# Causal attention on one Trainium2 core: the diagonal blocks become a unit of their own, with their masks on other engines

## The chip, the cores and the metric

The kernel runs on one core of a Trainium2 chip. The metric is the device time of one execution in microseconds (us). The core has a matmul engine (TensorE, "PE" in the profile, its weight loads "PEld"), three engines for elementwise work (VectorE "DVE", ScalarE "ACT", GpSimd "POOL") and queues that start DMA transfers ("SPq" is the one of SyncE). [...]

## The reference, cut to what matters

The program has four stages on x of 8 batches x 1024 tokens x 256 features: a banded attention, a mixture of experts, a causal attention ("attn_b"), and the experts again. Only the causal attention is touched:

```python
def _L0_attn_b_ref(x, W1, b1, W2, b2):
    y = jnp.einsum('bse,ef->bsf', x, W1) + b1            # B 8, S 1024, H 16 heads of 16
    y = y.reshape(B, S, H, -1).transpose(0, 2, 1, 3)
    q, k, v = jnp.split(y, 3, axis=-1)
    w = jnp.einsum('bhqd,bhkd->bhqk', q, k) / dk
    w = w * mask - NEG_BIG * (1.0 - mask)                # mask = tril
    w = jax.nn.softmax(w, axis=-1)
    attn = jnp.einsum('bhqk,bhkd->bhqd', w, v)
    ...
    return jnp.einsum('bse,ef->bsf', attn, W2) + b2
```

## The kernel before

The causal attention is `dense_attention`. It works in groups of 4 heads (HG), 4 groups a batch, 32 groups in all. The 1024 x 1024 scores of a head are 8 x 8 tiles of 128 x 128, of which 36 matter. They are packed in "units" of 1024 columns, so that each unit fills one PSUM slot: five units for a head (the fifth, of 512 columns, is shared by two heads), 18 slots' worth for a group. `unit_tiles` says which key tiles lie in a unit of the transposed scores ("S"), `unit_maxima` which query tiles lie in a unit of the maxima pass ("mx").

Each group runs two passes over the scores. "mx" (L1193) computes queries x keys, so that VectorE's TENSOR_REDUCE (L1334) finds each query's maxima by tile. "mred" (L1304 to L1314) reduces these and splits the result in three bf16 parts, "mt" transposes them on TensorE (L1250), VectorE copies them (L1347), and "mrow" sends them by DMA (L1143) to three extra rows of `q_stack`. Then "S" (L1186) computes keys x queries minus the maximum, ScalarE takes the exponential (L1373) into `probs`, and "PV" (L1213) multiplies the values with them into `outT_ps`. PV's four heads write to four different groups of 17 of the array's columns; it is fp32, and each matmul has two records. In both passes every diagonal tile gets its mask by one more 128-column bf16 matmul that adds -1e30: `sooner` in S (L1189), `later` in mx (L1198).

The order of all work is one written-out list, `dense_schedule`. A group is 18 "beats"; each has one S step, up to one or two PV pieces, then the mx steps of the *next* group (18 of them spread over beats 0 to 14), and side work. "mred" is at beat 15, "mt" and "mrow" at beat 16. Side work by group of a batch: group 0 has the output of the batch before (ot, at, op: beats 4 to 8) and the layer norm and transposes of the next one (z, zt: beats 10 to 13), groups 1 and 3 project q and k of the next batch (from beat 6), group 2 its values. Every engine walks the list in order and skips what isn't its own.

S, mx and the side work share a ring of three PSUM slots (`slot_free`): a step may write when the step three before it has been taken out by VectorE or ScalarE. A projection's slot is taken twice: by ScalarE, which adds the bias and rounds to bf16 (L1387, part 0), and then by VectorE, which forms the remainder in `full` (L1341). ScalarE rounds that to part 1 (L1391), VectorE subtracts again for part 2 (L1319), and SyncE spills the three parts to DRAM, from where they are stacked.

A PV piece of unit u is put in the list from the first S step of unit u+1 on, one a beat, and its matmuls wait for the last exponential of unit u.

Of the kernel before, what the change touches and what calls it, by code (L numbers as in the profile page):

```python
# [844 lines left out]

UNITS = 5
# [5 lines left out]
def unit_tiles(u):  # L852

    return ((u, 0), (NT - u, N - P * u)) if 0 < u < 4 else ((0, 0),) if u == 0 else ((4, 0),)


def unit_maxima(u):

    return ((7 - u, 0), (u - 1, P * (NT - u))) if 0 < u < 4 else ((7, 0),) if u == 0 else ((3, 0),)


def dense_schedule():

# [16 lines left out]
    def maxima(b, g):  # L880
# [21 lines left out]
    def others(b, g):  # L902
# [25 lines left out]
    for b in range(B):  # L928
        for g in range(G):
# [5 lines left out]
            for n, step in enumerate(beat_units("S", b, g)):  # L935
# [5 lines left out]
                for _ in range(1 if u < 4 else 2):  # L941
# [10 lines left out]
def dense_attention(nc, x_sb, stats, ident, w, scratch):  # L952
# [4 lines left out]
    for name, kinds in {"filled": BY_DVE + BY_ACT, "taken_dve": BY_DVE, "taken_act": BY_ACT, "qk": ("q", "k"), **{kind: (kind,) for kind in (  # L957
            "S", "PV", "ote", "z", "mred", "part1", "part2", "mrow")}}.items():
# [29 lines left out]
    with ExitStack() as ctx:  # L988
# [11 lines left out]
        sooner = sb("sooner", [P, P], BF16)  # L1000
# [4 lines left out]
        with ExitStack() as setup:  # L1005
# [8 lines left out]
            with nc.Block() as block:  # L1014
# [20 lines left out]
                def _(pool):  # L1035
# [3 lines left out]
                    pool.memset(sooner[:, :], 0.0).then_inc(pool_steps, 1)  # L1039
                    pool.wait_ge(pool_steps, 3)  # L1040
# [5 lines left out]

                    pool.affine_select(out=sooner[:, :], in_=sooner[:, :], compare_op=ALU.is_ge, fill=NEG, base=0,
                                       pattern=[[1, P]], channel_multiplier=-1).then_inc(pool_steps, 1)
                    pool.wait_ge(pool_steps, 6)
# [29 lines left out]
        tops = sb("tops", [P, HG, 4 * NT + NT // 2])  # L1079
        neg_max = sb("neg_max", [P, HG, NT])  # L1080
# [11 lines left out]
        pv_done, ote_done, z_ready, mred_chain, mred_done, recip_done = (  # L1092
            sem(n) for n in ("pv_done", "ote_done", "z_ready", "mred_chain", "mred_done", "recip_done"))
        part0_done, part1_done, part2_done, mrows_in = (sem(n) for n in ("part0_done", "part1_done", "part2_done", "mrows_in"))
# [781 lines left out]
```

## Time and profile before

| | us |
|---|---|
| median of 3 runs | 3950.71 (3942.34 to 3953.79) |
| the profiled execution | 3953.15 |
| its span | 3951.4 |
| TensorE busy | 3270.7 (83%) |
| VectorE busy | 1763.2 (45%) |
| ScalarE busy | 1195.8 (30%) |
| GpSimd busy | 77.1 (2%) |

In the page's slices of the span, the causal attention is the second half up to about 3600 us, which starts at 1990 us; its steady part is 2030 to 3580 us. A busy time counts a matmul from its start to its modelled end, so that matmuls that follow each other closely overlap: the cost of one in a stream is read from start to start. "Idle before" is the time that the engine stood still ahead of a group of instructions, with what ended it.

### The profile page before, as it was taken

The page shows a single profiled execution, that of the slowest core. Times are in us where ns is not written, and L with a number is a line of the kernel's source. Part 1 is how long each engine was busy: PE and PEld are TensorE (multiplying, and loading weights), DVE is VectorE, ACT ScalarE, POOL GpSimd, SP SyncE. Part 2 cuts the span into 40 slices and gives each one's busy share as a digit, 9 for nine tenths or more (in the row PEclk, how much of TensorE's full clock was granted, in tenths as well). Part 3 has the DMA queues.
Part 4 walks back from the last instruction along what each step waited for, and adds up shares of the span by engine and source line. Part 5 has one row for each costly group of instructions (what it writes and reads, how often), then busy time and mean ns, then how long its engine had stood idle before and what let it go on. Part 6 is the DMA issues. An engine that isn't in the chain of part 4 may idle for free. (4 is left out here: it accounts for less than half of the span.)

```text
span 3951.4 us, 96618 instructions
## 1 busy us (share of the span) xinstructions
PE 3270.7 (83%) x43580; PEld 1868.0 (47%) x43580; DVE 1763.2 (45%) x3275; ACT 1195.8 (30%) x1486; POOL 77.1 (2%) x144
## 2 busy tenths in 40 slices
PE   1688888888888888789758888888888888887898
PEld 0466566656565656434524434343434343443345
DVE  5233343434333434430555555555555655563402
ACT  0122222222222222231024444444444444443300
POOL 0000000000000000000000000000000000000000
PEclk9678798878888878899679999999999999998997
DMA  5422223232223232239232222222222222202295
GB/s 129 101 68 68 71 71 79 65 82 62 74 62 79 58 81 61 90 140 415 57 80 49 49 49 49 49 49 49 49 49 49 49 49 49 49 17 89 82 418 186
DMA packets 235030, 343.13 MB, mean 87 GB/s; under 512 B 115962, under 2 KB 144452, under 8 KB 218244
## 3 DMA queue, kind: packets, MB, share of 16 engines
q1 hardware_dynamic: 222452, 334.40, 29.6%
q8 instruction: 340, 5.57, 0.6%
q10 hardware_dynamic: 12176, 2.66, 0.5%
q14 instruction: 62, 0.51, 0.0%
HBM read 266.15 MB, written 69.24 MB: 85 GB/s over the span
## 5 line engine op out<-in xcount | busy, mean ns | idle before, releaser
L1334 DVE TENSOR_REDUCE b_tops<-b_slot 128x8 f32<-128x1024 f32 x576 | 688.6, 1220 | 489.3 <-PE b_slot L1198 482.4
L1373 ACT ACTIVATE b_probs<-b_slot 128x1024 f32<-128x1024 f32 x576 | 584.1, 1022 | 581.1 <-PE b_slot L1189 396.2
L1186 PE MATMUL b_slot<-b_q_stack,b_k_stack 99*128 99x512 bf16 (+3 forms) x1536 | 389.8, 335 | 131.6 <-DMA b_q_stack<-b_neg_rows 71.2
L711 DVE TENSOR_TENSOR a_probs<-a_scores,a_bias_k 128x512 f32<-128x512 f32 x256 | 176.6, 690 | 559.5 <-PE a_scores L570 325.4
L1193 PE MATMUL b_slot<-b_k_stack,b_q_stack 96*128 96x512 bf16 (+3 forms) x1536 | 382.5, 341 | 30.5 <-DVE b_tops L1334 22.1
L1213 PE MATMUL b_outT_ps<-b_probs,b_v 128*17 128x512 f32 (+3 forms) x3072 | 333.3, 514 | 22.2 <-ACT b_probs L1373 22.2
L803 ACT ACTIVATE a_probs<-a_probs 128x512 f32<-128x512 f32 x256 | 161.5, 631 | 592.6 <-DVE a_probs L711 591.4
L1186 PEld LDWEIGHTS b_slot<-b_q_stack,b_k_stack 99*128 99x128 bf16 x1536 | 138.4, 100 | 299.9 <-DMA b_q_stack<-b_neg_rows 93.9
L1193 PEld LDWEIGHTS b_slot<-b_k_stack,b_q_stack 96*128 96x128 bf16 x1536 | 120.3, 100 | 291.2 <-issue 174.5
L1189 PE MATMUL b_slot<-b_sooner,b_ident 128*128 128x128 bf16 x1024 | 227.5, 222 | 0.0
L1198 PE MATMUL b_slot<-b_later,b_ident 128*128 128x128 bf16 x1024 | 209.0, 223 | 0.0
L1747 PE MATMUL f_ps<-f_w_ring,f_hidT 128*32 128x256 f32 x1024 | 184.0, 381 | 2.1 <-ACT f_hidT L1788 2.1
L576 PE MATMUL a_aux<-a_k_stack,a_q_stack 96*64 96x64 bf16 x2048 | 162.2, 313 | 8.1 <-issue 8.1
L631 PE MATMUL a_outT_ps<-a_probs,a_v_near 128*17 128x64 f32 (+1 forms) x8448 | 164.8, 239 | 4.5 <-issue 4.4
L576 PEld LDWEIGHTS a_aux<-a_k_stack,a_q_stack 96*64 96x64 bf16 x2048 | 138.1, 219 | 50.2 <-issue 50.1
L658 PE MATMUL a_aux<-a_zT,a_wqk 128*128 128x512 f32 x256 | 159.6, 782 | 0.8 <-ACT a_zT L831 0.8
L576 PE MATMUL a_scores<-a_q_stack,a_k_stack 99*64 99x64 bf16 x2048 | 159.7, 313 | 0.0
L631 PEld LDWEIGHTS a_outT_ps<-a_probs,a_v_near 128*17 128x17 f32 x8448 | 143.1, 110 | 27.5 <-issue 18.3
L1726 PE MATMUL f_ps<-f_w_ring,f_lhs 128*32 128x512 f32 x512 | 146.8, 601 | 7.9 <-POOL f_lhs L1710 7.9
L763 DVE TENSOR_REDUCE a_far_max<-a_aux 128x8 f32<-128x512 f32 x128 | 88.4, 692 | 137.3 <-PE a_aux L576 137.3
L651 PE MATMUL a_aux<-ident,a_zb 128*128 128x128 f32 x128 | 28.5, 369 | 140.3 <-DVE a_zb L719 140.3
L576 PEld LDWEIGHTS a_scores<-a_q_stack,a_k_stack 99*64 99x64 bf16 x2048 | 137.1, 219 | 13.7 <-issue 4.1
(211 smaller groups left out, 4126.0 us busy)
## 6 DMA issues: line engine op xcount, KB each, us to landing
f_w_ring<-in_L_ffn_w_dram SPq DMA_DIRECT2D x128, 1024.0 KB, 9.4
parts_dram<-a_parts SPq DMA_DIRECT2D x96, 256.0 KB
parts_dram<-b_parts SPq DMA_DIRECT2D x96, 256.0 KB
a_k_stack<-parts_dram SPq DMA_DIRECT2D x128, 128.0 KB, 3.0
b_k_stack<-parts_dram SPq DMA_DIRECT2D x64, 256.0 KB, 6.9
a_q_stack<-parts_dram SPq DMA_DIRECT2D x64, 192.0 KB, 3.0
b_q_stack<-parts_dram SPq DMA_DIRECT2D x32, 384.0 KB, 4.7
values_dram<-a_v_stage SPq DMA_DIRECT2D x32, 272.0 KB, 2.9
```

The costliest lines, as they stand in the source:

```text
L576: ins = pe.matmul(dst[RES * r2:RES * (r2 + 1), 64 * pair:64 * (pair + 1)], left[rows, h, r:N:LINKS], right[rows, h, r:N:LINKS], start=star ...
L631: ins = pe.matmul(outT_ps[BLK * h:BLK * h + HD + 1, lo:top], v_near[g % 2][:, c, blk % 4, (HD + 1) * h:(HD + 1) * (h + 1)], probs[h][:, at ...
L711: dve.tensor_tensor(dst[:, :].rearrange("p (t c) -> p t c", c=64), src[:, :].rearrange("p (t c) -> p t c", c=64), bias_k[k][:, HG * g + h, ...
L803: act.activation(dst[:, :], dst[:, :], ACT.Exp).then_inc(probs_ready, 1)
L1186: ins = pe.matmul(dst[:, at:at + top - lo], k_stack[n][:, head, mine], q_stack[n][:, head, lo:top], start=True, stop=not own, skip_group_c ...
L1189: ins = pe.matmul(dst[:, at:at + P], ident16[:, :], sooner[:, :], start=False, stop=True, skip_group_check=True)
L1193: ins = pe.matmul(dst[:, at:at + top - lo], q_stack[n][0:QK_ROWS, head, mine], k_stack[n][0:QK_ROWS, head, lo:top], start=True, stop=not o ...
L1198: ins = pe.matmul(dst[:, at_own:at_own + P], ident16[:, :], later[:, :], start=False, stop=True, skip_group_check=True)
L1213: ins = pe.matmul(outT_ps[32 * h:32 * h + HD + 1, lo:hi], v1[b % 2][:, j, HG * g + h, :], src[:, base + lo - P * j:base + hi - P * j], sta ...
L1334: ins = dve.tensor_reduce(out, src, AX.X, ALU.max)
L1373: act.activation(probs_of(b, g, u, h)[:, :], slot_of(step)[:, :], ACT.Exp).then_inc(taken_act, 1)
L1747: ins = pe.matmul(bank[4 + half][32 * j:32 * j + 32, 0:D], hidT[half][:, c, j, :], w2_ring[:, j, c, :], start=c == 0, stop=c == HE // P - 1)
```

## The change

The units of both passes are cut anew. Unit 0 is now the eight diagonal tiles of a head, side by side; units 1 to 4 hold only tiles off the diagonal (in S unit 1 holds key tiles 0 and 6, and so on). What follows from it:

- S has no mask matmuls. In its unit 0 GpSimd sets what lies above the diagonal to zero in `probs`, after the exponential, with one affine_select of 128 x 1024 for each head; PV pieces of unit 0 wait for these ("masked").
- mx has its masks in unit 0 alone: two matmuls of 512 columns with `later` broadcast, ahead of the eight blocks. The reduction by tile gives diagonal and other maxima apart, and mred joins them with one more instruction.
- PV of unit 0 is 8 tiles x 4 heads of 128 columns, in two pieces. PV pieces come one at each beat but a unit's first (in the last unit, one and two).
- The 18 mx steps are spread over beats 0 to 12, mred is at beat 13, mt and mrow at 15.
- A projection's slot is taken once, by VectorE, into `full` (with the bias). ScalarE rounds `full` to part 0, GpSimd subtracts it from `full` ("rest1"), ScalarE makes part 1, GpSimd part 2. Projections start at beat 5, with six steps for each of q and k, where it was 6 with four.
- VectorE waits for all memsets once, ahead of its first step.

The diff, cut:

```diff
 def unit_tiles(u):
-    return ((u, 0), (NT - u, N - P * u)) if 0 < u < 4 else ((0, 0),) if u == 0 else ((4, 0),)
+    return ((u - 1, 0), (7 - u, N - P * u)) if u < 4 else ((3, 0),)
 def unit_maxima(u):
-    return ((7 - u, 0), (u - 1, P * (NT - u))) if 0 < u < 4 else ((7, 0),) if u == 0 else ((3, 0),)
+    return ((NT - u, 0), (u, N - P * u)) if u < 4 else ((4, 0),)
...
-            out += [(which, b, half), ("part1", b, half, which), ("part2", b, half, which), ("spill", b, half, which)]
+            out += [(which, b, half)] + [(step, b, half, which) for step in ("part0", "rest1", "part1", "part2", "spill")]
...
-            out[n * (BEATS - 3) // len(units)].append(step)
-        out[BEATS - 3].append(("mred", b, g))
-        out[BEATS - 2] += [("mt", b, g), ("mrow", b, g)]
+            out[n * (BEATS - 5) // len(units)].append(step)
+        out[BEATS - 5].append(("mred", b, g))
+        out[BEATS - 3] += [("mt", b, g), ("mrow", b, g)]
...
+        if u == 0:
+            return [("PV", b, g, 0, n, 512 * n, 512 * n + 512) for n in range(2)]
...
-            for lo, hi in ((P * j, 512), (max(512, P * j), N)):
+            for lo, hi in ((P * (j + 1), 512), (max(512, P * (j + 1)), N)):
...
-                put(projections(b + 1, g // 2), 6)
+                put(projections(b + 1, g // 2), 5)
...
-                for _ in range(1 if u < 4 else 2):
+                for _ in range((h > 0) if u < 4 else 1 + h):
...
+                for step in seq:
+                    if step[0] == "S" and step[3] == 0:
+                        _, b, g, u, h = step
+                        pool.wait_ge(taken_act, count("taken_act", *step))
+                        blocks = probs_of(b, g, u, h)[:, :].rearrange("p (j q) -> p j q", q=P)
+                        pool.affine_select(out=blocks, in_=blocks, compare_op=ALU.is_ge, fill=0.0, base=0,
+                                           pattern=[[0, NT], [1, P]], channel_multiplier=-1).then_inc(masked, 1)
+                    elif step[0] == "rest1":
+                        pool.wait_ge(part0_done, count("part0", "part0", b, half, which))
+                        pool.tensor_tensor(full[:, :], full[:, :], parts["qk".index(which)][:, 0, :], ALU.subtract).then_inc(rest1_done, 1)
+                    elif step[0] == "part2":
+                        pool.wait_ge(part1_done, count("part1", "part1", b, half, which))
+                        pool.tensor_tensor(parts[m][:, 2, :], full[:, :], parts[m][:, 1, :], ALU.subtract).then_inc(part2_done, 1)
...
+                        if u == 0:
+                            for c in range(2 if kind == "mx" else 0):
+                                pe.matmul(dst[:, 512 * c:512 * (c + 1)], ident16[:, :], later[:, :].unsqueeze(1).to_broadcast([P, 4, P]),
+                                          start=True, stop=False, skip_group_check=True)
+                            for tile in range(NT):
+                                mine = slice(P * tile, P * tile + P)
+                                ins = pe.matmul(dst[:, mine], own[0:rows, h, mine], other[0:rows, h, mine], start=kind == "S", stop=True,
+                                                skip_group_check=True)
...
-                                        if own:
-                                            ins = pe.matmul(dst[:, at:at + P], ident16[:, :], sooner[:, :], start=False, stop=True,
-                                                            skip_group_check=True)
...
+                        if u == 0:
+                            pe.wait_ge(masked, HG * (b * G + g + 1))
...
+                dve.memset(neg_off[:, :, :], -LOWEST).then_inc(cleared, 1)
+                dve.wait_ge(cleared, N_CLEARED)
...
-                        for u in range(UNITS):
+                        for u in range(1, UNITS):
...
+                        dve.wait_ge(mred_chain, n + 1)
+                        dve.scalar_tensor_tensor(out=neg_max[:, :, :], in0=tops[:, :, 0:NT], scalar=-1.0, in1=neg_off[:, :, :],
+                                                 op0=ALU.mult, op1=ALU.min).then_inc(mred_chain, 1)
...
-                            dve.wait_ge(part0_done, count("qk", *step))
-                            ins = dve.scalar_tensor_tensor(out=full[:, :], in0=src[:, :], scalar=bqk[:, m, half:half + 1],
-                                                           in1=parts[m][:, 0, :], op0=ALU.add, op1=ALU.subtract)
+                            ins = dve.tensor_scalar(full[:, :], src[:, :], bqk[:, m, half:half + 1], None, ALU.add)
...
+                        act.wait_ge(taken_dve, count("taken_dve", which, b, half))
+                        act.activation(parts[m][:, 0, :], full[:, :], ACT.Copy).then_inc(part0_done, 1)
```

## Rows read from the trace of the kernel before

**Rows 1.** Busy time in stretches: us, PE, PEld, DVE, ACT, POOL, PEclk, DMA share, GB/s

```profile
1990.00:2032.00 42.00, 29.38 (x88) 16.00 (x88) 13.15 (x17) 13.73 (x13) 0.00 (x0) 0.78 0.36 87
...
2030.00:3520.00 1490.00, 1282.72 (x8956) 594.27 (x8956) 856.20 (x1186) 666.75 (x662) 0.00 (x0) 0.96 0.23 50
```

**Rows 2.** Waits of PE from 2030 to 3520 us: total, times, longest

```profile
PE b_slot L1186 <- DMA b_q_stack<-b_neg_rows: 67.4, 30, 3.2
PE b_slot L1186 <- DVE b_full L1341: 42.9, 28, 1.5
PE b_slot L1193 <- DVE b_tops L1334: 21.7, 76, 0.4
PE b_outT_ps L1213 <- ACT b_probs L1373: 17.6, 36, 0.6
PE b_slot L1186 <- DVE b_tops L1334: 15.7, 39, 0.5
...
PE b_slot L1250 <- DVE b_neg_parts L1314: 12.7, 8, 4.3
```

**Rows 3.** Timeline of PE, 2602 to 2604 us: start, length, instruction

```profile
2602.39 0.22 PE L1198 MATMUL b_slot<-b_later,b_ident 128*128 128x128 bf16 x1
2602.45 0.22 PE L1193 MATMUL b_slot<-b_k_stack,b_q_stack 96*128 96x128 bf16 x1
...
2603.13 0.38 PE L1186 MATMUL b_slot<-b_q_stack,b_k_stack 99*128 99x512 bf16 x1
2603.34 0.22 PE L1189 MATMUL b_slot<-b_sooner,b_ident 128*128 128x128 bf16 x1
```

**Rows 4.** Timeline of PE around two value products, 2614 to 2617 us

```profile
2614.22 1.05 PE L1213 MATMUL b_outT_ps<-b_probs,b_v 128*17 128x512 f32 x8
...
2615.21 0.50 PE L1193 MATMUL b_slot<-b_k_stack,b_q_stack 96*128 96x512 bf16 x2
...
2616.42 0.41 PE L1213 MATMUL b_outT_ps<-b_probs,b_v 128*17 128x128 f32 x8
...
2616.76 0.45 PE L1193 MATMUL b_slot<-b_k_stack,b_q_stack 96*128 96x512 bf16 x2
```

**Rows 5.** Timeline of DVE: the first maxima alone, then a remainder and mred

```profile
2033.34 20.45 DVE L1334 TENSOR_REDUCE b_tops<-b_slot 128x8 f32<-128x1024 f32 x18 [7.25 <-PE b_slot L1198]
...
2622.84 1.28 DVE L1341 SCALAR_TENSOR_TENSOR b_full<-b_slot,b_bqk,b_parts 128x1024 f32<-128x1024 f32 x1 [2.96 <-PE b_slot L1198]
...
2631.38 0.72 DVE L1304 TENSOR_REDUCE b_neg_max<-b_tops 128x4 f32<-128x32 f32 x8
```

**Rows 6.** Timeline of PE: after a projection, then a group's end and the next start

```profile
2624.18 0.39 PE L1186 MATMUL b_slot<-b_q_stack,b_k_stack 99*128 99x512 bf16 x1 [1.53 <-DVE b_full L1341]
...
2629.65 0.38 PE L1193 MATMUL b_slot<-b_k_stack,b_q_stack 96*128 96x512 bf16 x1
...
2631.75 1.27 PE L1213 MATMUL b_outT_ps<-b_probs,b_v 128*17 128x128 f32 x16 [0.56 <-ACT b_probs L1373]
2633.04 0.26 PE L1250 MATMUL b_slot<-b_ident,b_neg_parts 128*96 128x128 bf16 x1
...
2636.73 0.61 PE L1186 MATMUL b_slot<-b_q_stack,b_k_stack 99*128 99x512 bf16 x1 [2.11 <-DMA b_q_stack<-b_neg_rows]
```

**Rows 7.** Timeline of ACT: a projection's part 0, then an exponential

```profile
2621.64 1.11 ACT L1387 ACTIVATE b_parts<-b_slot,b_bqk 128x1024 bf16<-128x1024 f32 x1 [4.09 <-PE b_slot L1231]
2622.65 1.02 ACT L1373 ACTIVATE b_probs<-b_slot 128x1024 f32<-128x1024 f32 x1
```

**Rows 8.** Groups of POOL over the whole span: busy us, mean ns, idle before

```profile
L490 POOL TENSOR_TENSOR a_far_parts<-a_spread,a_far_parts 128x256 bf16<-128x256 f32 x32 | 21.4, 670 | 2.6
...
L107 POOL TENSOR_SCALAR_AFFINE_SELECT ident<-ident 128x128 f32<-128x128 f32 x1 | 0.3, 295 | 0.2 <-POOL ident L105 0.2
```

**Rows 9.** Stretches of PE before and after a group's start: us, busy, PEclk, DMA share, GB/s

```profile
2634.00:2636.00 2.00, 0.62 (x8) 1.00 0.27 89
...
2638.00:2640.00 2.00, 2.00 (x9) 0.50 0.96 200
```

More of the change, by code:

```diff
@@ L957, in dense_attention @@
     for name, kinds in {"filled": BY_DVE + BY_ACT, "taken_dve": BY_DVE, "taken_act": BY_ACT, "qk": ("q", "k"), **{kind: (kind,) for kind in (
-            "S", "PV", "ote", "z", "mred", "part1", "part2", "mrow")}}.items():
+            "S", "PV", "ote", "z", "mred", "part0", "rest1", "part1", "part2", "mrow")}}.items():
         for step in seq:
@@ L1038, in _ @@
                     pool.memset(later[:, :], 0.0).then_inc(pool_steps, 1)
-                    pool.memset(sooner[:, :], 0.0).then_inc(pool_steps, 1)
-                    pool.wait_ge(pool_steps, 3)
+                    pool.wait_ge(pool_steps, 2)
                     pool.affine_select(out=ident16[:, :], in_=ident16[:, :], compare_op=ALU.not_equal, fill=1.0, base=0,
@@ L1045, in _ @@
                                        pattern=[[-1, P]], channel_multiplier=1).then_inc(pool_steps, 1)
-                    pool.affine_select(out=sooner[:, :], in_=sooner[:, :], compare_op=ALU.is_ge, fill=NEG, base=0,
-                                       pattern=[[1, P]], channel_multiplier=-1).then_inc(pool_steps, 1)
-                    pool.wait_ge(pool_steps, 6)
+                    pool.wait_ge(pool_steps, 4)
                 @block.scalar
@@ L1175, in _ @@
                         dst = slot_free(step)
-                        heads = ((h, 0),) if u < 4 else ((2 * h, 0), (2 * h + 1, 512))
-                        for head, base in heads:
+                        own, other, rows = (k_stack[n], q_stack[n], ALL_ROWS) if kind == "S" else (q_stack[n], k_stack[n], QK_ROWS)
+                        if u == 0:
[6 more added lines that the diff above has]
+                                                skip_group_check=True)
@@ L1178, in _ @@
+                        for head, base in ((h, 0),) if 0 < u < 4 else ((2 * h, 0), (2 * h + 1, 512)) if u else ():
                             for tile, at in (unit_tiles if kind == "S" else unit_maxima)(u):
                                 at += base
-                                mine = slice(P * tile, P * tile + P)
-                                lo, end = (P * tile, N) if kind == "S" else (0, P * tile + P)
+                                lo, end = (P * tile + P, N) if kind == "S" else (0, P * tile)
@@ L1200, in _ @@
+                                    ins = pe.matmul(dst[:, at:at + top - lo], own[0:rows, head, P * tile:P * tile + P],
+                                                    other[0:rows, head, lo:top], start=True, stop=True)
                                     at, lo = at + top - lo, top
@@ L1203, in _ @@
                         _, b, g, u, n, lo, hi = step
-                        first = step == ("PV", b, g, 0, 0, 0, 512)
-                        pe.wait_ge(taken_act, count("taken_act", "S", b, g, u, HG - 1 if u < 4 else HG // 2 - 1))
-                        if first:
+                        begins = u == 0 and n == 0
+                        if u == 0:
+                            pe.wait_ge(masked, HG * (b * G + g + 1))
+                        else:
+                            pe.wait_ge(taken_act, count("taken_act", "S", b, g, u, HG - 1 if u < 4 else HG // 2 - 1))
+                        if begins:
                             if prev := before(b, g):
@@ L1314, in _ @@
                         dve.tensor_tensor(neg_parts[:, 2, :, :], neg_max[:, :, :], neg_parts[:, 1, :, :], ALU.subtract).then_inc(mred_done, 1)
-                    elif kind == "part2":
-                        _, b, half, which = step
-                        m = "qk".index(which)
-                        dve.wait_ge(part1_done, count("part1", "part1", b, half, which))
-                        dve.tensor_tensor(parts[m][:, 2, :], full[:, :], parts[m][:, 1, :], ALU.subtract).then_inc(part2_done, 1)
                     elif kind == "stats":
```

60 lines of the change are left out of this document (26 added, 34 removed).

## Prediction

> **What bounds the kernel now.** I read the busy times by stretch first, to see which engine is nearest to full in the causal attention. From 2030 to 3520 us TensorE is busy 1283 of 1490 us, VectorE 856, ScalarE 667, GpSimd not at all [rows 1]. So TensorE's own work and its idle time set this stage, and the other stages are untouched. Then I read the waits of TensorE: what stopped it, by releaser [rows 2]. The largest is the start of a group, where S waits for the DMA that brings the negated maxima: 67.4 us in 30 groups, 2.25 us each. Next is the slot of a projection, which two engines take out in turn: 42.9 us, 28 times 1.53 us. Then the slot ring, where a step waits for VectorE's reduction of the step three before: 21.7 + 15.7 = 37.4 us, 1.2 us a group. The first value product of a unit waits for an exponential: 17.6 us. The transpose of the maxima waits for mred: 12.7 us, of which the first group has 4.3 and seven others 1.2 each.
>
> Third, the timeline, for what an instruction costs in a stream (start to start, not its length). A mask of 128 columns starts at 2602.39 and the next matmul at 2602.45: 0.06 us. A block of 512 columns takes 0.21 (2603.13 to 2603.34) [rows 3]. A PV piece of four heads takes 0.99 us for 512 columns and 0.34 for 128 [rows 4]. By these, each group has 18 S steps, 18 mx steps and twelve PV pieces on TensorE. VectorE's reductions back to back take 20.45/18 = 1.14 us each [rows 5], so the 18 of a group need 20.5 us of the 46 that a group lasts.
>
> Fourth, the granted clock. TensorE's clock is at 2.4 GHz most of the time, but the wait at a group's start is followed by a stretch at 1.2 GHz: 1.00 at 2634 to 2636 us, 0.50 at 2638 to 2640, where a step's 512 columns took 0.61 us in length instead of 0.38 [rows 3, 6, 9]. The mean over the stage is 0.96 [rows 1], so some 0.08 of 1490 us, 119 us, run at half speed and lose about 60 us. It isn't every group that falls.
>
> **The change part by part.** All of it is in 32 groups. Own time of the profiled execution: 3953.15 us.
>
> *S.* For each head it loses eight masks (8 x 0.06) and the two 512-column blocks of key tile 0 (2 x 0.215), and gains eight blocks of 128 (8 x 0.06); the other blocks have the same widths as before. Net 0.43 us a head, x 128 heads = **-55 us**. mx has the same number of blocks and masks by column: eight 128-column masks become two of 512, two 512-column blocks become eight of 128. That is 0 on TensorE, but it gathers the masks in the first four mx steps, which then take 0.91 us (2 x 0.215 + 8 x 0.06), the others 0.44.
>
> The Trainium skill, page "TensorE: Matmul & The Clock Gate", section "Back-to-back issue gap", speaks against small blocks: it states a sustained 81 ns for a matmul of 128 columns with its weight load and 131 for one of 512. By its figures S would save only 2 x 0.131 a head, 34 us, and the forecast would stand at 3873. The trace shows 0.06 and 0.21 us [rows 3] and decides.
>
> *PV of the diagonal.* Two 512-column pieces (1.98 us) become eight tiles of 128 columns for four heads. Each of these takes 0.34 us as such a piece does now [rows 4], 2.72 in all, +0.74 a group = **+24 us**. If the loads of the tiles hide behind each other, only columns count, (0.99 - 0.34)/3 = 0.22 a tile, 1.73 in all, -8 us. I take 0.34, since it is the same matmul at the same width.
>
> *Start of a group.* mt (2633.04) to the next group's S (2636.73) is 3.69 us [rows 6]: transpose, copy, DMA. mt moves from one beat before the end to two. Behind it TensorE then has two S steps (0.88) and PV pieces of 128, 512 and 384 columns (0.34 + 0.99 + 0.77, the last by the same slope), 3.0 us in all. The wait becomes 0.7 where it was 2.25: -1.55 x 31 = **-48 us**. mrow is one DMA on SyncE's queue; a projection's k spill (three DMAs), ahead of it before, is now behind it, and the stacking after that is for a group that starts 40 us later.
>
> *The maxima in time for mt.* From the last mx step to mt, TensorE does three S steps and pieces of 256, 512 and 256 columns, 1.3 + 2.1 = 3.4 us. VectorE needs 0.2 + 1.14, then mred: 1.65 us as now (2631.38 to 2633.04 less the hand-over) [rows 5, 6], less one reduction of 0.09, plus the joining instruction at about 0.2. That is 3.1 us if it has no backlog, so most groups wait 0 to 0.5, say 0.2 in 24 groups = 5. In group 0 of a batch the layer norm falls in beats 10 and 12 and VectorE is behind: I take 2 us more in seven groups, 14. Together **+19 us**.
>
> *A projection's slot.* TensorE's S step waited 1.53 us for ScalarE's 1.11 and VectorE's 1.28 in turn [rows 6, 7, 5]. Now VectorE alone takes it, and the q step has a PV piece of the diagonal behind it that covers the rest. Of 42.9 us I leave 6: **-37 us**. The chain behind it has GpSimd in it twice: subtractions of 1024 elements, by the row of 256 (670 ns) [rows 8] between 2.4 us (if 0.1 of it is fixed, my assumption) and 2.7. From part 0 to part 1 lie two beats of some 1.5 us, so ScalarE, whose exponentials queue behind part 1, waits about nothing; q's part 2 is out before k's `full` is needed five beats on. Before the first group nothing covers it: q and k in turn take 1.28 + 1.02 + 2.4 + 1.02 + 2.4 = 8.1 us each where they took about 4.6, overlapped, and the maxima start about **+8 us** later.
>
> *Value products one beat later.* The 17.6 us for exponentials go: **-17 us**. The cover of the diagonal's masks is the same stretch, and is worked out below.
>
> *The slot ring.* The 18 mx steps now lie in 13 beats, and the first beats have no PV piece in four of five. I stepped through beats 0 to 5 at full clock with S 0.44, mx of unit 0 0.91, other mx 0.44, a reduction from 0.2 us after the fill at 1.14 each, an exponential 1.02, a slot free 0.1 later. TensorE starts S0 at 0, mx0 0.44, mx1 1.33, S1 2.22, PV 2.66, mx2 3.64, S2 4.53, mx3 4.97, mx4 5.95, S3 6.39, mx5 7.28, S4 8.42, mx6 8.86, ot 9.56, S5 10.50, PV of the diagonal 10.94. That has 1.5 us of stalls, all for VectorE's reductions, since seven of them (8.0 us) stand against 8.1 us of TensorE's work. Double mx steps in beats 5, 7 and 10 add about 1.5 in groups with little side work, and none where outputs or values fill the beats. I take 2.2 us a group where it is 1.2 now [rows 2]: **+32 us**. Ends: 0, and +106 if VectorE sets the pace all through the 13 beats (2.3 us more a group).
>
> *Masks on GpSimd.* The affine_select isn't in the trace at this width. At 128 columns it takes 295 ns [rows 8]; with the same 0.1 fixed that is 1.5 ns a column, 1.7 us for 1024. Ends: 1.0 us (most of the 295 fixed) and 2.4 (the slope of the two-input row). Four run for a group, the last when exp of S3 is out at 8.05, and the diagonal's PV is reached at 10.94: 8.05 + 1.8 is in time. Cost **0**.
>
> *The clock.* A wait of 0.7 us where 2.25 stood should bring fewer falls, but the ring's stalls bring others. Of the 60 us I take **-25**, ends 0 and -50.
>
> Sum: -55 + 24 - 48 + 19 - 37 + 8 - 17 + 32 - 25 = -99 us. 3953.15 - 99 = 3854; the median is 2.4 below the profiled execution, so 3852.
>
> **The rivals.**
>
> *VectorE becomes the bound* in beats 0 to 12: ring at +106 in place of +32. For it: 20.5 us of reductions beside some 21 us of TensorE's own work there. Against: side work of 10 us a group on TensorE, most in these beats. 3926. Chance 0.10.
>
> *The wait only moves*: mt waits for mred in every group by what the S step waited before, since mred is late by the same backlog: the 48 and the 25 aren't gained. 3925. Chance 0.08.
>
> *Slower: the masks are late.* If an affine_select of [8, 128] elements takes T, the fourth is done at 1.8 + 4T + 0.1, and TensorE stands at the diagonal's PV from T = 2.26 us on. It eats the whole gain (3.1 us a group) at T = 3.04. At 3.3 us it is 4.2 us x 32 = +133: 3985. For it: the only row is 128 columns wide, on a one-level pattern. Against: even the two-input row gives 2.4, which would cost 0.6 us a group, 3870. Chance 0.08.
>
> *GpSimd and VectorE hold each other up.* mred's subtractions and joining, all from SBUF, fall in beat 13, where k's rest1 runs in 14 groups; if one waits for the other's end, mt is late by up to 2.4 us, 34 us: 3886. No row here shows it: GpSimd's subtractions of the banded stage took 670 ns on the mean of 32 [rows 8]. Chance 0.08. The Trainium skill, page "SBUF — State Buffer", section "Who interferes with whom", states that a VectorE instruction with two SBUF inputs contends with a GpSimd instruction that reads SBUF; no run here shows it yet.
>
> *Small blocks cost more than their columns* (the weight load shows): 20 us less gained, 3873. Chance 0.04.
>
> *All clock falls go and the ring is no tighter*: -32 and -25 more, 3795. Chance 0.10.
>
> **How the numbers follow.** The forecast has 0.52, with a range of its own of 3805 to 3900 (PV -8 to +24, ring 0 to +106, clock 0 to -50). The range 3795 to 3930 leaves out the slower case, half of the best one and tails. A difference of 0.3% (12 us) is about what a measurement of this kernel tells from none. Faster: all but the slower case, less 0.3 of the two cases near 3925 and tails, 0.83. Same 0.07, slower 0.10.
>
> **What would show it.** Right: no matmul with sooner left on TensorE; waits of S for the maxima's DMA near 20 us where 67 stood; of L1341's kind below 10 (VectorE taking a projection); affine_select near 1.7 us, and PV never waiting for it; reductions' waits near 70 us; a granted clock of 0.97 or more over the stage; PV starts in unit 0 of 0.34 us apart by tile. Wrong: TensorE waiting for POOL at PV; mt waiting for mred in most groups by over 1 us; VectorE instructions of mred that are several times longer than 0.2 us; or 128-column blocks spaced at over 0.06 us.

## The result, and the profile after

The changed kernel takes 3780.8 us (median of 4 runs, 3777.1 to 3786.6) where the kernel before takes 3946.5; the ratio is 0.9581, with a 95% interval of 0.9558 to 0.9605. That is 166 us less. The prediction said 3852, 99 us less, with a range that ended at 3795: the sign was right, and the gain came out two thirds larger. The profiled execution took 3782.0 us, its span 3780.3.

First, where the time went. The causal attention runs from VectorE's first layer-norm instruction (1990.4 us before, 1981.6 after) to the first statistics of the next experts (3622.1 and 3449.7): 1631.7 us before, 1468.1 after, -163.6. The 8.8 us by which it begins sooner belong to the stages ahead of it, whose code is the same; among the executions shown below this start lies between 1966 and 1990 us, so comparisons below are made inside the stage where they are finer than the medians.

The steady part, from the first DMA of the maxima to the last, as busy time by stretch (columns as in [rows 1]; the first row is the kernel before, the second the changed one):

```profile
2056.10:3565.10 1509.00, 1309.05 (x9198) 604.97 (x9199) 863.16 (x1203) 690.09 (x685) 0.00 (x0) 0.96 0.22 47
```

```profile
2054.80:3399.40 1344.60, 1219.08 (x10421) 602.38 (x10421) 852.21 (x1175) 683.24 (x684) 254.95 (x180) 0.99 0.25 53
```

It is 164.4 us shorter. TensorE's busy time falls by 90 and its idle time from 200 to 126, and the granted clock rises from 0.96 to 0.99. Added up from the trace's clock records, the stretches at half clock (1.2 GHz) in this part are 109 us before and 33 after; TensorE is busy in 95 and 30 us of them. The waits of TensorE in that stretch of the changed kernel, which answer to [rows 2]:

```profile
PE b_slot L1208 <- DVE b_tops L1351: 50.8, 120, 0.5
PE b_slot L1238 <- DVE b_zb L1312: 20.7, 14, 1.8
PE b_slot L1246 <- DVE b_tops L1351: 8.6, 14, 0.6
PE b_slot L1200 <- DMA b_q_stack<-b_neg_rows: 8.6, 16, 3.3
PE b_slot L1208 <- DVE b_full L1357: 7.1, 14, 0.5
PE b_slot L1265 <- DVE b_neg_parts L1336: 6.7, 14, 0.5
...
PE b_slot L1272 <- DVE b_tops L1351: 5.3, 30, 0.2
```

The wait for the DMA of the maxima, 67.4 us in [rows 2], is 8.6, of which 3.3 is the first group alone. The slot ring (the three lines with b_tops) is now the largest; a slot lies in PSUM, the memory into which TensorE writes its results and from which VectorE and ScalarE take them. Next is the wait for the layer norm of the next batch (b_zb), 20.7 us where it was 14.7. The end of a group on TensorE, which answers to [rows 6]:

```profile
2270.99 0.26 PE L1265 MATMUL b_slot<-b_ident,b_neg_parts 128*96 128x128 bf16 x1
...
2272.50 1.70 PE L1228 MATMUL b_outT_ps<-b_probs,b_v 128*17 128x512 f32 x16
2274.50 0.62 PE L1200 MATMUL b_slot<-b_q_stack,b_k_stack 99*128 99x128 bf16 x8 [0.30 <-DMA b_q_stack<-b_neg_rows]
2274.96 0.60 PE L1196 MATMUL b_slot<-b_later,b_ident 128*128 128x512 bf16 x2
```

The way from mt (L1265) to S (L1200) is still 3.5 us. Two S steps and three value products now fill 3.2 of it (the last two products are the line at 2272.50), and the rest is 0.3. Behind it the S step of eight diagonal blocks takes 0.46 us start to start, at full clock; the same place before ran at half clock [rows 6, 9].

The diagonal's value products, one piece of 4 tiles x 4 heads, 1.00 us start to start (before, a 512-column piece took 0.99 [rows 4]):

```profile
2590.07 1.07 PE L1228 MATMUL b_outT_ps<-b_probs,b_v 128*17 128x128 f32 x32
2591.07 1.04 PE L1208 MATMUL b_slot<-b_k_stack,b_q_stack 96*128 96x512 bf16 x6
```

Inside the piece the four heads of a tile start within 0.02 us of each other, and the next tile 0.22 us later.

GpSimd's groups over the span, which answer to [rows 8] (columns: busy us, mean ns, idle before):

```profile
L1155 POOL TENSOR_SCALAR_AFFINE_SELECT b_probs<-b_probs 128x1024 f32<-128x1024 f32 x128 | 139.8, 1093 | 809.5 <-ACT b_probs L1388 809.5
```

Its two subtractions of 1024 columns (L1160, L1165) take 2.13 us each.

### The profile page after: what moved, and what is told of

Its sections match the earlier page's. It is cut to its first block and busy times, and to the rows that moved or that the text cites. A ratio compares the mean times of both kernels' runs of the same rounds, so it can differ in the third digit from the quotient of the medians.

```text
span 3780.3 us, 99336 instructions
## 1 busy us (share of the span) xinstructions
PE 3176.4 (84%) x44860; PEld 1864.3 (49%) x44860; DVE 1747.6 (46%) x3244; ACT 1189.4 (31%) x1486; POOL 352.9 (9%) x334
## 5 line engine op out<-in xcount | busy, mean ns | idle before, releaser
L1351 DVE TENSOR_REDUCE b_tops<-b_slot 128x8 f32<-128x1024 f32 x576 | 680.4, 1220 | 361.5 <-PE b_slot L1208 182.6
L1228 PE MATMUL b_outT_ps<-b_probs,b_v 128*17 128x128 f32 (+3 forms) x4608 | 318.0, 384 | 6.2 <-ACT b_probs L1388 5.5
L1208 PE MATMUL b_slot<-b_q_stack,b_k_stack 99*128 99x512 bf16 (+3 forms) x1280 | 275.8, 322 | 43.3 <-DVE b_tops L1351 32.8
L1208 PE MATMUL b_slot<-b_k_stack,b_q_stack 96*128 96x512 bf16 (+3 forms) x1280 | 267.1, 323 | 29.4 <-DVE b_tops L1351 20.6
L1155 POOL TENSOR_SCALAR_AFFINE_SELECT b_probs<-b_probs 128x1024 f32<-128x1024 f32 x128 | 139.8, 1093 | 809.5 <-ACT b_probs L1388 809.5
L1208 PEld LDWEIGHTS b_slot<-b_q_stack,b_k_stack 99*128 99x128 bf16 x1280 | 107.2, 100 | 204.6 <-DVE b_tops L1351 61.9
L1208 PEld LDWEIGHTS b_slot<-b_k_stack,b_q_stack 96*128 96x128 bf16 x1280 | 97.6, 98 | 185.4 <-DVE b_tops L1351 61.6
L482 POOL TENSOR_TENSOR a_spread<-a_far_max,a_among 128x256 f32<-128x256 f32 x32 | 21.4, 669 | 1414.6 <-DVE a_far_max L763 1414.6
L1228 PEld LDWEIGHTS b_outT_ps<-b_probs,b_v 128*17 128x17 f32 x4608 | 96.3, 96 | 113.5 <-issue 69.3
L658 PE MATMUL a_aux<-a_zT,a_wqk 128*128 128x512 f32 x256 | 151.1, 745 | 0.8 <-ACT a_zT L831 0.8
```

Source lines behind the costliest of these rows:

```text
L658: ins = pe.matmul(dst[:, :], wqk[:, "qk".index(kind), kd, 8 * half:8 * half + 8, :].rearrange("p h d -> p (h d)"), zT[:, kd, c * 512:(c + ...
L1155: pool.affine_select(out=blocks, in_=blocks, compare_op=ALU.is_ge, fill=0.0, base=0, pattern=[[0, NT], [1, P]], channel_multiplier=-1).the ...
L1208: ins = pe.matmul(dst[:, at:at + top - lo], own[0:rows, head, P * tile:P * tile + P], other[0:rows, head, lo:top], start=True, stop=True)
L1228: ins = pe.matmul(outT_ps[32 * h:32 * h + HD + 1, first:last], v1[b % 2][:, j, HG * g + h, :], src[:, base + first:base + last], start=u = ...
L1351: ins = dve.tensor_reduce(out, src, AX.X, ALU.max)
```

## The experiments

Three questions were open: which part of the change gave more than its terms; how the parts depend on each other; and whether the rivals' conditions (late masks, dear small blocks, VectorE as the bound) were near. Each time is a median, each ratio is against the kernel before on the same chip. The chips differ a little (the kernel before took 3938 to 3950 us), so what one kernel costs against another is taken from the ratios, times 3947 us; the intervals leave such a difference open by 10 to 30 us. "Steady part" is the stretch used above, in the one execution whose trace was kept, and "half clock" the sum of that trace's stretches at 1.2 GHz in it.

### 1. The maxima's placement, undone in the changed kernel and done alone in the one before

```diff
-            out[n * (BEATS - 5) // len(units)].append(step)
-        out[BEATS - 5].append(("mred", b, g))
-        out[BEATS - 3] += [("mt", b, g), ("mrow", b, g)]
+            out[n * (BEATS - 3) // len(units)].append(step)
+        out[BEATS - 3].append(("mred", b, g))
+        out[BEATS - 2] += [("mt", b, g), ("mrow", b, g)]
```

> The changed kernel (3781 us) with one part undone: the 18 maxima steps over beats 0 to 14, mred at 15, mt and mrow at 16, as before the change. Theory A (the placement of the maxima is the largest single part, and was sized too small): the wait of S for the DMA of the maxima comes back to 60 to 70 us, the slow-clock time after it comes back (30 to 40 us), and the ring's waits fall by some 15, so about 3860 us. Theory B (the terms of the prediction were right for this part: -48, -25 and +51 for ring and late mred, and the surplus lies elsewhere): about 3805 us.

Measured: 3830.8 us, ratio 0.9702 (0.9654 to 0.9751). The same lines the other way round in the kernel before:

> The kernel before (3947 us) with this one part alone: the 18 maxima steps over beats 0 to 12, mred at 13, mt and mrow at 15. Theory A: 70 to 85 us less, near 3868. Theory B: about 22 us less, near 3925. If this gives much less than undoing it in the changed kernel costs, the part needs another one (shorter S steps) to work.

Measured: 3898.1 us, ratio 0.9882 (0.9827 to 0.9937). Both lie between the two theories: the placement is worth 48 and 47 us, more than twice the 22 of the prediction's terms together, and less than theory A. What TensorE waited for with the old placement in the changed kernel:

```profile
PE b_slot L1265 <- DVE b_neg_parts L1336: 52.8, 31, 2.3
PE b_slot L1200 <- DMA b_q_stack<-b_neg_rows: 28.8, 26, 3.3
```

Part of the wait stands at mt now, which I read as shorter S steps bringing TensorE to mt too soon after mred: 53 + 29 us, against 6.7 + 8.6. The ring gives back 30 us of that (L1208 waits 20.8 us for b_tops where it was 50.8), and half clock is 98 us where it was 33. In the kernel before with the new placement alone, the wait for the DMA did not go away; it was 39.4 us in 16 waits, all at the end of groups 1 and 3 but for the first group's (3.3) and one of 0.2. There mt to S took 5.4 to 6.7 us, in the other groups no wait was left. Something in groups 1 and 3, which have the projections, held up the DMA.

### 2. The projections' chain of before, in the changed kernel

```diff
-            out += [(which, b, half)] + [(step, b, half, which) for step in ("part0", "rest1", "part1", "part2", "spill")]
+            out += [(which, b, half), ("part1", b, half, which), ("part2", b, half, which), ("spill", b, half, which)]
...
-                put(projections(b + 1, g // 2), 5)
+                put(projections(b + 1, g // 2), 6)
...
-                            ins = dve.tensor_scalar(full[:, :], src[:, :], bqk[:, m, half:half + 1], None, ALU.add)
+                            dve.wait_ge(part0_done, count("qk", *step))
+                            ins = dve.scalar_tensor_tensor(out=full[:, :], in0=src[:, :], scalar=bqk[:, m, half:half + 1],
+                                                           in1=parts[m][:, 0, :], op0=ALU.add, op1=ALU.subtract)
```

> The changed kernel with the projections' chain of before: ScalarE forms part 0 from the slot, VectorE the remainder and part 2, four steps from beat 6. Theory A (the second taker of the slot costs TensorE its full wait of 1.5 us, 28 times): 30 to 40 us more, near 3816. Theory B (a value product of the diagonal behind the q step now covers half of it, and VectorE's extra 1.2 us a projection is free): 15 to 20 us more, near 3798.

Measured: 3851.2 us, ratio 0.9748 (0.9699 to 0.9798): 66 us more than the changed kernel, some twice what theory A gave and four times theory B. The slot's wait came back as expected (43.6 us, 28 times), and that explains about half. In the steady part, which is 88 us longer (the traced execution took 3862 us, the longest of its four), the slot's wait is 36 us more, that for the maxima's DMA 36 more (44.8), and half clock 130 us where it was 33, which costs 46; the ring gives back 19. Why the DMA is late is in the timeline. SyncE's queue and TensorE at the end of a group 1:

```profile
2130.09 1.90 SPq L1126 DMA_DIRECT2D parts_dram<-b_parts  x3
2132.31 0.99 SPq L1143 DMA_DIRECT2D b_q_stack<-b_neg_rows  x1
```

```profile
2131.77 0.26 PE L1256 MATMUL b_slot<-b_ident,b_neg_parts 128*96 128x128 bf16 x1 [0.23 <-DVE b_neg_parts L1327]
2137.85 1.03 PE L1191 MATMUL b_slot<-b_q_stack,b_k_stack 99*128 99x128 bf16 x8 [2.88 <-DMA b_q_stack<-b_neg_rows]
```

The spill of k, three DMAs of 256 KB, has been issued 0.3 us before the small DMA of the maxima starts to be, and mt to S takes 6.1 us in place of 3.5 (5.8 to 6.1 in twelve of these groups, 4.4 and 4.8 in two). S then runs at half clock (eight blocks in 1.03 us of length, 0.62 in the changed kernel). In the changed kernel the order is the other way round, since k's chain has six steps and its spill falls in beat 16, behind mrow:

```profile
2134.68 0.76 SPq L1143 DMA_DIRECT2D b_q_stack<-b_neg_rows  x1
2136.48 1.91 SPq L1126 DMA_DIRECT2D parts_dram<-b_parts  x3
```

### 3. The spill's place alone

One edit, on three kernels: k's spill at beat 16 and not 13.

```diff
-                put(projections(b + 1, g // 2), 6)
+                put(projections(b + 1, g // 2)[:-1], 6)
+                out[BEATS - 2] += projections(b + 1, g // 2)[-1:]
```

> a_chain_old (3851 us) with k's spill moved from beat 13 to 16, behind the DMA of the maxima on SyncE's queue; nothing else. Theory A (of the 70 us that the old chain cost, about half is the spill's three DMAs ahead of that DMA: in groups 1 and 3 it took 5.9 us from mt to S where 3.5 is usual, 2.5 us in each of 14 groups, and the slow clock behind these waits): S's wait for the maxima falls from 45 to under 12 us, and 45 to 55 us are gained, 3800. Theory B (the old chain costs by its slot and by VectorE's longer queue alone): no change, 3851.

Measured: 3810.2 us, ratio 0.9666 (0.9639 to 0.9692), and S's wait for the maxima 15.1 us where it was 44.8. That is theory A's cause, at 32 us by the ratios and not its 45 to 55. What the old chain costs beside the spill is then the rest, 0.9666 against 0.9581, 34 us. The prediction had 37 for the slot, but the two agree by more than the slot: in the steady part (42 us longer than the changed kernel's) the slot's wait is 36 us more and half clock, 87 us where it was 33, costs 26, while the ring gives back 18.

> b_maxima_new (3898 us: the kernel before with the maxima placed sooner) with k's spill moved from beat 13 to 16. Theory A: its remaining wait for the maxima's DMA, 39 us in 16 groups, falls to about 5, and slow-clock time with it: 35 to 50 us less, near 3855. Theory B: no change, 3898.

Measured: 3841.5 us, ratio 0.9751 (0.9729 to 0.9773), 52 us less by the ratios, the upper end of theory A. The waits for the DMA are 4.8 us in all. The stretch:

```profile
2036.70:3456.70 1420.00, 1271.46 (x9178) 1.00 0.24 50
```

Half clock is 8 us, at the first group alone, where it was 62 without the later spill (columns: us, PE busy, PEclk, DMA share, GB/s). Two edits of the schedule in the kernel before, with none of the new units, masks or chain, give 97 us of the 166.

> A control on the kernel before (3947 us): k's spill moved from beat 13 to 16, the maxima where they were (mt and mrow at 16). Theory A (the spill costs only where the maxima's DMA is issued right behind it; in the kernel before the two were three beats apart and mt to S took 3.3 to 3.8 us in groups 1, 2 and 3 alike): within 12 us of 3947, S's wait for the maxima still 65 to 72 us. Theory B (the spill's place is worth 40 to 55 us by itself, as in b_maxima_new_late and a_chain_old_late): 3895.

Measured: 3944.4 us, ratio 1.0007 (0.9986 to 1.0027), the wait for the DMA 70.1 us. The spill's place is worth nothing while the maxima's DMA is issued three beats behind it, and about 50 us (0.9882 to 0.9751) or 32 (0.9748 to 0.9666) once it stands right behind. The two are one measure. In the control the maxima's DMA is issued just ahead of the spill (2123.78 and 2124.65 us at the end of a group 1). Not tried is the spill on another engine's queue, so whether the small DMA is held up by its place in SyncE's queue or by the bytes in flight on the DMA engines is not shown.

### 4. The units cut anew, without placement and chain

The edits of experiments 1 and 2 together, applied to the changed kernel.

> The change without its two schedule parts: units cut anew, masks of S on GpSimd, masks of the maxima in unit 0, value products one beat later; but the maxima's placement and the projections' chain as before. The prediction's terms for this: S -55, diagonal's value products +24, exponentials -17, that is -48, near 3895 us. By what the changed kernel's trace shows (a tile of four heads 0.25 us and not 0.34): -55 + 1 - 17 = -71, 3870.

Measured: 3853.5 us, ratio 0.9779 (0.9719 to 0.9840). The median is 87 us below the kernel before of its chip, with an interval of 63 to 111; its steady part is 1434.1 us, 75 shorter. That is the 71 of the second reckoning rather than the 48 of the prediction. TensorE's busy time falls by 57 (54 reckoned for S and the value products) and the waits for exponentials by 19 (17). Beside these the ring's waits fell from 44 to 20 us, which neither reckoning had; the waits at a group's start (83 us where they were 78) and small ones took about as much back. It is also about as fast as the kernel of experiment 2, which has the new placement too (1432.2 us; 12 us by the ratios, within the intervals): with the spill ahead of it, the new placement took the waits for mred and the DMA from 83 to 48 us, but the ring rose from 20 to 46.

### 5. Value products: order and time

The diagonal's loops swapped, heads outside and tiles inside:

```diff
-                        for j, at in [(4 * n + i, 512 * n + P * i) for i in range(4)] if u == 0 else [unit_tiles(u)[n]]:
-                            ...
-                            for h in range(HG):
+                        tiles = [(4 * n + i, 512 * n + P * i) for i in range(4)] if u == 0 else [unit_tiles(u)[n]]
+                        for h in range(HG):
+                            for j, at in tiles:
```

> The changed kernel (3781 us) with the loops of the diagonal's value products swapped: each head's four tiles after each other, not four heads of a tile. Theory A (a tile of four heads took 0.25 us, not 0.34, because the four heads write to different columns of the array and run side by side, their loads under each other's matmuls; tiles of one head in a row can't): a piece of 16 matmuls goes from 1.0 us to about 3.4 (16 x 0.21), +2.4 x 64 = +150 us, near 3930. Theory B (the order doesn't matter, only the columns in sum): 3781.

Measured: 3852.6 us, ratio 0.9784 (0.9758 to 0.9810), 80 us more by the ratios, about half of theory A. The piece of 1.07 us became

```profile
2614.49 2.41 PE L1229 MATMUL b_outT_ps<-b_probs,b_v 128*17 128x128 f32 x32
```

so the order does decide, though each matmul, head by head, costs about 0.15 us and not 0.21.

Products from a unit's first beat on:

```diff
-                for _ in range((h > 0) if u < 4 else 1 + h):
+                for _ in range(1 if u < 4 else 2):
```

> The changed kernel with value products from a unit's first beat on (one a beat, two in the last unit), as before. The prediction says that the later place is worth the 17 us of waits for exponentials; here the diagonal's products also wait for GpSimd (exponential of the last head, then 1.1 us of affine_select). Theory A: 25 to 50 us more than 3781, with waits of TensorE for POOL. Theory B (the ring has less stalls when every beat has a piece, which pays for it): within 10 us.

Measured: 3809.4 us, ratio 0.9659 (0.9594 to 0.9724), some 30 more (26.7 in the steady part), which is theory A's size but not its cause: TensorE waited for GpSimd once for 2.6 us, at the last group, and otherwise 0.1 us at most. It waited for exponentials at products (10.9 us in 30) and at slots (10.5 in 35), and longer for mred at mt (14.4). These are 22 us more than in the changed kernel, less 5 that the DMA's wait loses. TensorE's busy time is 10 us longer as well, and why stays open.

### 6. Two rivals, tried

The affine_select done twice for each head:

> The changed kernel with GpSimd's affine_select done twice for each head (the second changes nothing): 2.2 us instead of 1.09. The prediction put the point from which TensorE waits at 2.26 us. Theory A (that is right, and the masks have 1.1 us of slack each): within 8 us of 3781. Theory B (the masks are nearly late already): each of 32 groups waits 1 us or more, 3815 and up.

Measured: 3774.7 us, ratio 0.9580 (0.9553 to 0.9607), no change. GpSimd masked twice at 1.09 us each for a head (2.18 us), 0.08 short of the point from which the prediction let TensorE wait. TensorE waited for it in two groups of 32: 1.3 us at the first and 4.6 at the last, which has no maxima steps beside its S steps.

The maxima without their masks:

```diff
-                            for c in range(2 if kind == "mx" else 0):
+                            for c in range(0):
...
-                                ins = pe.matmul(..., start=kind == "S", stop=True,
+                                ins = pe.matmul(..., start=True, stop=True,
```

> The changed kernel without the two mask matmuls of 512 columns in each first maxima step. The maxima of diagonal tiles are then taken over later keys too, so what is subtracted is an upper bound of each query's maximum; the softmax divides it out. Theory A (TensorE sets the pace): 0.43 us x 128 heads = 55 us less, near 3726. Theory B (VectorE's reductions set the pace in the first beats of a group, seven of 1.14 us against then 6.4 us of TensorE): most of it turns into waits for VectorE, 10 to 25 us less, near 3763.

Measured: 3742.3 us, ratio 0.9484 (0.9437 to 0.9531). The steady part is 1311.5 us, 33 shorter than the changed kernel's (38 by the ratios), of 55 that TensorE's work loses. TensorE's busy time fell by 47 and its idle time rose by 14. Of the 14, about 6 are waits for VectorE's reductions and 7 for ScalarE's exponentials at the diagonal's S steps, so neither theory holds: the gain is between them, and VectorE alone doesn't take the rest. This kernel also asks something of its inputs that the changed one doesn't: a later key's score far above all the visible ones would make the query's exponentials vanish. Then the double maxima steps in beats that have a value product:

```diff
-            out[n * (BEATS - 5) // len(units)].append(step)
+            out[(0, 1, 1, 2, 3, 4, 5, 5, 6, 6, 7, 8, 9, 9, 10, 10, 11, 12)[n]].append(step)
```

> a_no_top_mask (3742 us) with the double maxima steps in beats 1, 5, 6, 9 and 10, which have a value product, where they are in 0, 2, 5, 7 and 10. Theory A (the ring's waits, 54 + 9 + 5 us, come from two reductions in a beat without a product): they fall by 15 to 30 us, near 3720. Theory B (VectorE's 8 us of reductions in the first beats are the bound however they lie): no gain.

Measured: 3729.5 us, ratio 0.9469 (0.9409 to 0.9529). The steady part is 8 us shorter (1303.4), and the ring's waits fell from 68 to 58 us, less than theory A's 15 to 30. The intervals of the two overlap, so this last step is not shown by the times; it is the fastest kernel found, 44 us below the changed one by the ratios.

## Why the prediction was right or wrong, point by point

The sign was right and the causes came out as written, but the size did not: 99 us were forecast and 166 measured. The steps that failed are terms of the sum. The diagonal's value products (+24, measured +1) and mt's wait for mred (+19, measured -2) are 44 of the 67 us; the wait for the maxima's DMA, the ring and the clock came out better by 13, 12 and 8, and other waits took 14 back. The forecast's own range, 3805 to 3900, let only the value products, the ring and the clock move, and 3795 added a rival's end. The two terms that it held fixed, mt and the wait for the DMA, missed by 34 us, more than the 14 by which 3781 lies below 3795.

| term | predicted | measured in the steady part |
|---|---|---|
| S without masks | -55 | not apart; with the next line -57, TensorE's busy time less the clock's part |
| diagonal's value products | +24 | 64 pieces at 1.00 against 0.99: +1 |
| exponentials | -17 | 18.7 to 5.3 us: -13 |
| wait for the maxima's DMA | -48 | 69.2 to 8.6 us: -61 |
| mt waits for mred | +19 | 8.4 to 6.7 us: -2 |
| projection's slot | -37 | 42.9 to 7.1 us: -36 |
| before the first group | +8 | 65.7 to 73.2 us: +8 (ahead of the steady part) |
| slot ring | +32 | 44.2 to 64.7 us: +20 |
| clock | -25 | TensorE busy at half clock 95 to 30 us, half of it lost: -33 |

Waits for the layer norm rose by 6 and small ones by 3. The sum of the right column without what lies before the first group, with S at its -55, is -170; the steady part lost 164. The 6 us between are not assigned. TensorE's busy time bears S out: it fell by 90, of which the clock is 33. That leaves 57, where 55 for S less 1 for the value products is 54.

**The signs and the mechanisms.** What bounds the kernel, the S masks, the slot's second taker, the wait at a group's start, the ring getting tighter and the masks being hidden all came out as written. The masks' price (1.09 us, near the low end of 1.0 to 2.4) made one wait of 0.6 us, at the last group. The subtractions took 2.13 us, below both ends of 2.4 to 2.7, and made no wait of TensorE by themselves.

**The diagonal's value products were priced by the wrong row.** A piece of 128 columns takes 0.34 us today, and the step took four tiles as four such pieces. But 0.34 holds about 0.12 us that a piece pays once. Four in a row start 0.22 us apart and pay it once: 4 x 0.22 + 0.12 = 1.00, what a 512-column piece costs. The slope of the same rows, the low end in the text at -8, was the nearer choice, but left the 0.12 out. It is 23 us of the miss.

**mt was given a backlog that isn't there.** The step added 2 us in group 0 for the layer norm in VectorE's queue; mt waited 0 there. In beats 4 to 13 of group 0 TensorE has the output projection, and I read it that VectorE catches up beside that. That is not tested, and the backlog is there with the old placement: in the changed kernel with mred at beat 15, mt waited 2.3 us at the end of group 0 and 1.1 at that of group 2. It is 21 us of the miss. What mt does wait, 0.48 us at the end of groups 1 and 3, has in part another cause; see below.

**The ring.** Its end was forecast well, 2.2 us a group for 2.1 measured. The start was too low: the 1.2 us a group left out what the steps of projections and outputs wait for reductions, and was 1.4 with these.

**The move of the spill was valued at nothing.** The step saw that the k spill goes from ahead of the maxima's DMA to behind it, and gave it no price, since in the kernel before it cost none. The price arises with the new placement: without the later spill, 14 groups would have kept waits (2.6 to 2.9 us in twelve, 1.2 and 1.6 in two). The forecast of -48 held only because the spill was moved too: the sum contained the right figure without its condition, and as far as the working goes that was luck. Experiments 2 and 3 show this.

**The clock.** The prediction took 60 us as lost, half of the time at half clock. But only what TensorE works in that time is stretched: 95 of 109 us, 47 lost. Of these 33 came back, where -25 stood. The half-clock stretches follow long waits. Before, 19 of 22 lie behind the waits for mred and the DMA at a group's start; in the changed kernel 7 of 8 lie behind one wait of 1.8 us in each batch, for the layer norm, and the eighth at the first group. One of the seven:

```profile
2439.25 1.47 PE L1238 MATMUL b_slot<-ident,b_zb 128*128 128x128 f32 x8 [1.82 <-DVE b_zb L1312]
```

The granted clock is 1.00 from 2436 to 2438 us and 0.50 from 2440 to 2443. I had let the ring's stalls cost clock too; with 51 us of them, of 0.5 us or less, no row shows that they do. Nor does every long wait bring a fall: the kernel before with both schedule edits has 28 waits of 1.5 us at the slot and 14 for the layer norm of up to 1.7, and no half clock in the steady part but at the first group. The old chain in the changed kernel, with the spill late, has 28 slot waits of up to 1.8 us, and 12 of its 17 half-clock stretches lie behind these. So the layer norm's wait, 20.7 us and nearly all the half clock that is left, is what stands next; no run tried to move it.

**Of the rivals**, "all clock falls go and the ring is no tighter" (3795) was nearest in time, but not in cause: the ring did get tighter, and a third of the half clock stayed. VectorE as the bound, small blocks dearer than their columns (0.46 us for eight) and late masks did not come. The one on GpSimd and VectorE did, at a fraction of its price. The joining instruction of mred at the end of a group 1, and GpSimd at that time:

```profile
2131.65 1.55 DVE L1326 SCALAR_TENSOR_TENSOR b_neg_max<-b_tops,b_neg_off 128x32 f32<-128x32 f32 x1
```

```profile
2131.01 2.14 POOL L1160 TENSOR_TENSOR b_full<-b_full,b_parts 128x1024 f32<-128x1024 f32 x1 [9.61 <-ACT b_parts L1402]
```

The instruction usually takes 194 ns (the median of 32). Here it took 1.55 us and ended 0.05 us after GpSimd's subtraction. So it is at the end of each of the 14 groups 1 and 3 whose subtraction is under way when it starts, and in none of the other 18; with the maxima's old placement it starts later in the subtraction, and takes 1.00 us, 14 times of 14, again to 0.05 us after the subtraction's end. In the kernel with the old chain, where GpSimd doesn't subtract, its mean is 192 ns:

```profile
L1317 DVE SCALAR_TENSOR_TENSOR b_neg_max<-b_tops,b_neg_off 128x32 f32<-128x32 f32 x32 | 6.2, 192 | 1.1
```

Behind it mt waits 0.48 us in 14 groups, 6.7 us. Not all of it is this: in the kernel with the old chain mt still waits 0.23 us in such groups, so that some 4 us are GpSimd's. The Trainium skill, page "SBUF — State Buffer", section "Who interferes with whom", has it that a VectorE instruction with two SBUF inputs contends with a GpSimd instruction that reads SBUF; the trace agrees. The page "TensorE: Matmul & The Clock Gate", section "Back-to-back issue gap", gives 81 ns for 128 columns and 131 for 512; here they take 0.06 and 0.21 us. The measurement decides, and S was worth its columns.

## What to carry to other kernels

A step that is moved ahead in a schedule is worth only what the queues in front of it allow: read which transfers are issued within a few microseconds ahead of a small, urgent one, and move these too. Where a row is used at another count, split it first into what is paid once and what is paid for each column. And when long waits of TensorE go, count the slow clock behind them: here it came to 33 us beside 110 us of waits.

## What the runs showed of the hardware

- A VectorE instruction of 0.19 us on 32 columns, both inputs in SBUF, that started during a GpSimd subtraction ended 0.05 us after it, 28 times of 28 in two kernels (it took 1.55 us in the changed one, 1.00 with the maxima's old placement).
- Four heads' fp32 value products, to four different column groups of the array, take 1.00 us for 16 matmuls of 128 columns in the order tile by tile (the four of a tile start within 0.02 us), and 2.4 in the order head by head.
- Behind three DMAs of 256 KB on the same queue, issued just before, a DMA of 24 KB let S start some 2.5 us later than usual (mt to S 6.1 against 3.5 us). Three beats behind them, or ahead of them, it was not held up (3.4 to 3.8 us).
- TensorE's clock fell to 1.2 GHz behind a single wait of 1.8 us, once in each of seven batches of the changed kernel; behind ring stalls of 0.5 us or less it did not.
- GpSimd's affine_select takes 1.09 us for 128 x 1024 fp32, 0.3 us for 128 columns (another pattern), and a subtraction of 1024 columns 2.13 us.
